# A statistics pass over scattered edge rows: all seven tile sums on TensorE, and six load buffers instead of four

## The reference, cut to what matters

```
def _bn(x, gamma, beta):
    mu = jnp.mean(x, axis=0)
    var = jnp.mean(jnp.square(x - mu), axis=0)
    return gamma * (x - mu) * jax.lax.rsqrt(var + EPS) + beta
z = jnp.concatenate([node_feats[src], node_feats[dst], edge_feats], axis=1)
gate = jax.nn.sigmoid(_bn(z @ W_int + b_int, g_int, be_int))
upd = jax.nn.softplus(_bn(z @ W_upd + b_upd, g_upd, be_upd))
agg = jax.ops.segment_sum(gate * upd, dst, num_segments=N_NODES)
```

## Time and profile before

| what | before |
|---|---|
| median of 3 runs | 12183.24 us |
| the profiled execution | 12194.69 us (span 12193.1) |
| busy over the span | DVE 75%, PE 65%, ACT 54%, POOL 42% |
| first to last v of the statistics stage (288 steps) | 3474.64 to 4572.85 us |
| in 3500 to 4500 us: DVE, PE, ACT busy of 1000 us | 955.6, 633.7, 585.1 us |
| in 3500 to 4500 us: granted TensorE clock, DMA | 1.00, 0.76 busy, 210 GB/s |

### The profile page before, as it was taken

The page is one execution under the profiler, slowest core; times in us unless marked ns, Lnnn a source line. Parts: engine busy times, 40 slices in busy tenths (PEclk is TensorE's granted clock), DMA queues, the critical chain, the costliest instruction groups (busy, mean ns, idle before and its releaser), DMA issues. The chain is left out here.

```text
span 12193.1 us, 449789 instructions
## 1 busy us (share of the span) xinstructions
PE 7964.7 (65%) x149683; PEld 7351.9 (60%) x149684; DVE 9105.9 (75%) x22324; ACT 6577.3 (54%) x15886; POOL 5172.2 (42%) x4482
## 2 busy tenths in 40 slices
PE   6444444388866667996676667667667676675865
PEld 6333333388854447886666666657666576665765
DVE  6777777578889999996785676875767757678367
ACT  1222222189965557995414545976458764588320
POOL 2777777634410001110360482643835527446044
PEclk8555555599999998997987867878678786787997
DMA  5555553289977777995994998969989799998897
GB/s 202 170 168 168 168 156 84 55 306 349 348 230 212 207 212 258 322 322 196 355 296 175 317 289 274 318 204 315 290 269 320 213 315 287 263 324 248 325 340 222
DMA packets 1409651, 3076.60 MB, mean 252 GB/s; under 512 B 389771, under 2 KB 1007813, under 8 KB 1398307
## 3 DMA queue, kind: packets, MB, share of 16 engines
q1 hardware_dynamic: 1034062, 2124.82, 50.1%
q0 software_dynamic: 331264, 823.09, 25.3%
q10 hardware_dynamic: 44116, 125.96, 3.4%
HBM read 1869.12 MB, written 1138.02 MB: 247 GB/s over the span
## 5 line engine op out<-in xcount | busy, mean ns | idle before, releaser
L2122 POOL DMA_INDIRECT mask_cols<-cols_all,mask_index x864 | 1372.5, 1589 | 1226.5 <-ACT mask_index L2131 1051.8
L539 POOL DMA_INDIRECT rows_s<-place_rec,place_index x1568 | 1635.7, 1043 | 538.5 <-issue 533.1
L614 PE MATMUL place_slot_ps<-place_runs,place_oh_turned 50*128 50x100 f32 x3136 | 725.9, 423 | 1236.8 <-DVE place_runs L653 1218.3
L614 PEld LDWEIGHTS place_slot_ps<-place_runs,place_oh_turned 50*128 50x128 f32 x3136 | 683.0, 327 | 1271.1 <-issue 1270.8
L2270 POOL DMA_INDIRECT hop_x<-cols_all,hop_index x864 | 976.2, 1130 | 1064.6 <-ACT hop_index L2277 741.2
L2286 ACT ACTIVATE hop_parts<-hop_x,mask 128x64 f32<-128x64 f32 x5184 | 1266.4, 335 | 51.0 <-DMA hop_x<-cols_all,hop_index 27.0
L2333 PE MATMUL hop_sums_ps<-hop_parts,hop_onehot 128*128 128x64 bf16 x18144 | 882.1, 216 | 470.3 <-DVE hop_parts L2315 394.3
L2333 PEld LDWEIGHTS hop_sums_ps<-hop_parts,hop_onehot 128*128 128x128 bf16 x18144 | 781.2, 113 | 573.6 <-issue 573.0
L1515 POOL DMA_DIRECT2D cm_onehot<-hot_d x288 | 152.1, 528 | 1978.1 <-POOLq L107 1180.2
L2180 PE MATMUL mask_part_ps<-mask_now,mask_turned 128*128 128x64 bf16 x18144 | 922.2, 233 | 33.2 <-issue 17.5
L2180 PEld LDWEIGHTS mask_part_ps<-mask_now,mask_turned 128*128 128x128 fp8e4 x18144 | 898.0, 125 | 38.1 <-issue 38.0
(11 more groups left out here) (411 smaller groups left out, 26855.7 us busy)
## 6 DMA issues: line engine op xcount, KB each, us to landing
cols_all<-att_in_rows SPq DMA_DIRECT2D x216, 896.0 KB
mask_onehot<-hot_s SPq DMA_DIRECT2D x216, 896.0 KB
cols_all<-hop_in_rows SPq DMA_DIRECT2D x216, 896.0 KB
hop_onehot<-hot_s SPq DMA_DIRECT2D x864, 224.0 KB
rows_all<-blank SPq DMA_DIRECT2D x72, 1808.0 KB
ct_u<-rows_all SPq DMA_DIRECT2D x288, 452.0 KB
cm_v<-rows_all SPq DMA_DIRECT2D x288, 448.0 KB
cm_onehot<-hot_d POOLq DMA_DIRECT2D x288, 448.0 KB
```

The source lines that it names most:

```text
L539: nc.gpsimd.indirect_dma_start(m.rows_s.rearrange("p n w -> (p n) w"), bass.IndirectOffsetOnAxis(index[:, j, t:t + 1], 0), rec[:, j, t, :] ...
L614: last = nc.tensor.matmul(slot_ps[b][:, t, 0:2 * NBK], oh_turned[:, b, t, :], runs[:, b, t, :], start=True, stop=True)
L2122: nc.gpsimd.indirect_dma_start(cols[:, n, :], None, table, bass.IndirectOffsetOnAxis(index[:, n, :], 0), compute_op=ALU.add).then_inc(arri ...
```

## The change

The sum of v goes to TensorE in full. `add_up` issues two identity products: tiles 0 to 3 (512 columns), and tiles 4 to 6 (384 columns), the latter into the first three of the same four places of one PSUM bank. VectorE's addition into `sum_acc` is gone, with its semaphore `summed` and the memset. `sum_acc` has four places instead of seven and is copied once from PSUM at the end, and `stage_gate_norm` sums four places of it. The loads go into six buffers of `u`, and the load for batch `it + 6` (instead of `it + 4`) waits for the same square. Six is not a multiple of the unrolling by four, so VectorE, ScalarE and SyncE go through `each12`; TensorE stays with `each4`.

```
-                    for c in range(BATCH):
-                        last = nc.tensor.matmul(ps[:, i, 0:2 * F], m.ones[:], acc[:, c, :], start=c == 0, stop=c == BATCH - 1)
+                    places = acc.shape[1]
+                    for c in range(places):
+                        last = nc.tensor.matmul(ps[:, i, 0:2 * F], m.ones[:], acc[:, c, :], start=c == 0, stop=c == places - 1)
...
-        u = sb("u", [P, 4, UW])
+        u = sb("u", [P, 6, UW])
...
+        came = [sem(f"came{n}") for n in range(6)]
+        total_ps = ctx.enter_context(nc.psum_tensor("ct_total_ps", [P, 512], fp32))[:].rearrange("p (c w) -> p c w", w=W)
...
-                    if isinstance(it, int):
-                        return
-                    sp.wait_ge(squared, it + 3)
-                    load(it + 4, i)
-                for i in range(4):
-                    load(i, i)
-                each4(sp, step)
+                    if look_ahead(it, 6):
+                        sp.wait_ge(squared, it + 3)
+                        load(it + 6, (s * 4 + i) % 6)
+                for n in range(6):
+                    load(n, n)
+                each12(sp, step)
...
-                nc.vector.memset(sum_acc[:], 0.0).then_inc(summed, 1)
...
-                def hots(it, i, k):
-                    dve.wait_ge(came[i], k * 16 + 16)
-                    dve.wait_ge(hot_stored[i], k * 16 + 16)
+                def hots(it, n, k):
+                    i = n % 4
+                    dve.wait_ge(came[n % 6], (k * 2 + n // 6) * 16 + 16)
+                    dve.wait_ge(hot_stored[i], (k * 3 + n // 4) * 16 + 16)
...
                     add_squares(it - 1, (i - 1) % 2)
-                    dve.wait_ge(valued, it + 3)
-                    dve.wait_ge(summed, it + 1)
-                    dve.sem_inc(gate, 1)
-                    nc.vector.tensor_tensor(sum_acc[:, 0:OWN, :], sum_acc[:, 0:OWN, :], v[:, i % 2, 0:OWN, :], ALU.add).then_inc(summed, 1)
...
                 dve.wait_ge(totaled, IT + 3)
-                nc.vector.tensor_copy(sum_acc[:, OWN:BATCH, :], total_ps)
+                nc.vector.tensor_copy(sum_acc[:], total_ps)
...
-                    nc.tensor.matmul(total_ps.rearrange("p c w -> p (c w)"), m.ident[:], v[:, j, OWN:BATCH, :].rearrange("p c w -> p (c w)"),
-                                     start=False, stop=False).then_inc(totaled, 1)
+                    nc.tensor.matmul(total_ps.rearrange("p c w -> p (c w)"), m.ident[:], v[:, j, 0:4, :].rearrange("p c w -> p (c w)"),
+                                     start=False, stop=False)
+                    nc.tensor.matmul(total_ps[:, 0:BATCH - 4, :].rearrange("p c w -> p (c w)"), m.ident[:],
+                                     v[:, j, 4:BATCH, :].rearrange("p c w -> p (c w)"), start=False, stop=False).then_inc(totaled, 1)
...
-                    sum_acc, square_acc = sb("sum_acc", [P, BATCH, 2 * F], ctx=stats), sb("square_acc", [P, BATCH, 2 * F], ctx=stats)
+                    sum_acc, square_acc = sb("sum_acc", [P, 4, 2 * F], ctx=stats), sb("square_acc", [P, BATCH, 2 * F], ctx=stats)
```

More of the change, by code:

```diff
@@ L1319, in stage_conv_stats @@
         v_ps = [ctx.enter_context(nc.psum_tensor(f"ct_v_ps{j}", [P, 8, W], fp32))[:, 0:BATCH, :] for j in range(2)]
[L1320 to L1325, removed]
+        came = [sem(f"came{n}") for n in range(6)]
+        hot_stored, turned_stored = sem4("hot_stored"), sem4("turned_stored")
+        hot, turn, turned_s, spread, valued, squared, added, totaled, gate = (sem(n) for n in (
+            "hot", "turn", "turned_s", "spread", "valued", "squared", "added", "totaled", "gate"))
+        total_ps = ctx.enter_context(nc.psum_tensor("ct_total_ps", [P, 512], fp32))[:].rearrange("p (c w) -> p c w", w=W)
         with nc.Block() as block:
@@ L1328, in _, with load, step @@
             def _(sp):
-                def load(it, i):
-                    sp.dma_start(u[:, i, :], m.rows_d[:, bass.ds(it, 1), :].rearrange("p b w -> p (b w)")).then_inc(came[i], 16)
-                def step(it, i, k, more, s):
+                def load(it, n):
+                    sp.dma_start(u[:, n, :], m.rows_d[:, bass.ds(it, 1), :].rearrange("p b w -> p (b w)")).then_inc(came[n], 16)
+                def step(it, s, i, k, more, _):
                     sp.wait_ge(hot, it + 1)
@@ L1354, in _ @@
                 nc.vector.memset(square_acc[:], 0.0).then_inc(added, 1)
-                nc.vector.memset(sum_acc[:], 0.0).then_inc(summed, 1)
                 nc.vector.memset(square[:, 1, :, :], 0.0).then_inc(added, 1)
-                def hots(it, i, k):
-                    dve.wait_ge(came[i], k * 16 + 16)
-                    dve.wait_ge(hot_stored[i], k * 16 + 16)
+                def hots(it, n, k):
+                    i = n % 4
+                    dve.wait_ge(came[n % 6], (k * 2 + n // 6) * 16 + 16)
+                    dve.wait_ge(hot_stored[i], (k * 3 + n // 4) * 16 + 16)
                     dve.sem_inc(gate, 1)
-                    nc.vector.tensor_tensor(onehot[:, i, :, :], b2(m.iota_p[:], BATCH), b3(u[:, i, C * W:C * W + C], P),
+                    nc.vector.tensor_tensor(onehot[:, i, :, :], b2(m.iota_p[:], BATCH), b3(u[:, n % 6, C * W:C * W + C], P),
                                             ALU.is_equal).then_inc(hot, 1)
@@ L1369, in add_squares, with step @@
                     nc.vector.tensor_tensor(square_acc[:], square_acc[:], square[:, j, :, :], ALU.add).then_inc(added, 1)
-                def step(it, i, k, more, s):
+                def step(it, s, i, k, more, _):
+                    n = s * 4 + i
                     if look_ahead(it, 2):
-                        hots(it + 2, (i + 2) % 4, k + (i + 2) // 4)
+                        hots(it + 2, (n + 2) % 12, k + (n + 2) // 12)
                     dve.wait_ge(spread, it + 1)
@@ L1377, in step @@
                     dve.sem_inc(gate, 1)
-                    nc.vector.tensor_tensor(v[:, i % 2, :, :], v_ps[i % 2][:], u[:, i, 0:C * W].rearrange("p (c w) -> p c w", w=W),
+                    nc.vector.tensor_tensor(v[:, i % 2, :, :], v_ps[i % 2][:], u[:, n % 6, 0:C * W].rearrange("p (c w) -> p c w", w=W),
                                             ALU.add).then_inc(valued, 1)
                     add_squares(it - 1, (i - 1) % 2)
-                    dve.wait_ge(valued, it + 3)
-                    dve.wait_ge(summed, it + 1)
-                    dve.sem_inc(gate, 1)
-                    nc.vector.tensor_tensor(sum_acc[:, 0:OWN, :], sum_acc[:, 0:OWN, :], v[:, i % 2, 0:OWN, :], ALU.add).then_inc(summed, 1)
                 hots(0, 0, 0)
                 hots(1, 1, 0)
-                each4(dve, step)
+                each12(dve, step)
                 add_squares(IT - 1, 1)
                 dve.wait_ge(totaled, IT + 3)
-                nc.vector.tensor_copy(sum_acc[:, OWN:BATCH, :], total_ps)
+                nc.vector.tensor_copy(sum_acc[:], total_ps)
             @block.scalar
@@ L1403, in turn_out, with step @@
                     nc.scalar.copy(turned[:, i, :, :], turn_ps[:], saturate=False).then_inc(turned_s, 1)
-                def step(it, i, k, more, s):
+                def step(it, s, i, k, more, _):
                     if more:
-                        turn_out(it + 1, (i + 1) % 4, k + (i + 1) // 4)
+                        turn_out(it + 1, (i + 1) % 4, k * 3 + s + (i + 1) // 4)
                     act.wait_ge(valued, it + 3)
@@ L1410, in step @@
                     act.sem_inc(gate, 1)
-                    nc.scalar.copy(m.map_d[:, bass.ds(it, 1)], u[:, i, C * W + C:UW])
+                    nc.scalar.copy(m.map_d[:, bass.ds(it, 1)], u[:, (s * 4 + i) % 6, C * W + C:UW])
                     nc.scalar.square(square[:, i % 2, :, :], v[:, i % 2, :, :]).then_inc(squared, 1)
@@ L1417, in _ @@
                 turn_out(0, 0, 0)
-                each4(act, step)
+                each12(act, step)
             @block.tensor
```

## The result

| | before | after |
|---|---|---|
| median | 12184.12 us (6 runs, 12174.13 to 12208.0) | 11989.67 us (6 runs, 11981.62 to 11995.35) |
| ratio to before | | 0.9838, 95% interval 0.9827 to 0.9848 |
| span of the profiled execution | 12193.1 us | 11980.0 us |
| first to last v of the stage | 3474.64 to 4572.85: 3.83 us a step | 3464.94 to 4360.51: 3.12 us a step |

The kernel is 194 us faster by the medians, 185 to 211 by the interval; 207 were forecast, to 11976 us. In the profiled executions the 287 steps from first to last v take 1098.2 - 895.6 = 202.6 us less. From the first load to the first v it is 0.2 us more (10.19 and 10.42), and from the last v to the multiplication by `bn_scale` behind the stage 2.3 less (14.48 and 12.18), in all 204.7 us less. The stage started 9.9 us earlier, though nothing ahead of it had changed.

The account below looks back on a forecast made before the run. The ring of four load buffers (3.77 us a step) was taken to bound, VectorE (3.62) close behind. A step of 3.11 saves 205.6 us, plus 1.1 at the end: 207 us, to 11976 us; range 11945 to 12055.

Parts of the forecast that it names:

- The ring of four: Four load buffers: a load waits for the square of four batches earlier, holding the step at 3.77 us or more.
- VectorE's new floor: VectorE's instructions in a step without the sum: 3.62 us falls to 3.01.
- TensorE's step: TensorE's work in a step: turn_in 0.39, spread 1.17 and add_up 1.49, in all 3.05 us.
- P: Time of one step of the stage: highest floor 3.05 plus 0.06, so 3.11 us; range 3.01 to 3.20.
- The store of the one-hot: A one-hot waits until its buffer, one of four, is stored: 3P >= 4.12 + L, giving 2.71 us a step.
- L: Time from issue of a one-hot's store to the start of its reader, taken as the load's 4.01 us.
- this rival: DMA engines or the one-hot's store become the bound: priced at 3.4 us a step, 123 us saved, chance 0.13.
- TensorE is the longest by a hair: After the change TensorE's 3.05 us a step stands just above VectorE's 3.01.
- one of the signs that I gave for being wrong on the mechanism: VectorE waiting for a DMA in front of the one-hot would show the mechanism wrong.
- DMA share: Busy share of the DMA engines in the stage after the change: 0.85 to 0.97 expected.
- the rival on TensorE's clock: TensorE partly at 1.2 GHz in the stage: at one half of the steps 4.58 us, 12398 us; chance 0.03.
- the 81 ns: Rival: TensorE's short products take 81 ns each in an unbroken stream: step 3.82 us, 3 us saved, chance 0.02.

Follow-up runs that it names:

- experiments 1 and 2: Changed kernel with VectorE's sum put back: 12125.45 us, ratio 0.995; kernel before with all sums on TensorE, still four load buffers: 12185.59 us, ratio 0.9998.
- experiment 4: Changed kernel without the 384-column product (tiles 4 to 6 unsummed) and with each one-hot stored one step earlier: 11940.89 us, ratio 0.9806 to the kernel before.
- experiment 3: Changed kernel without the 384-column product, so tiles 4 to 6 are missing from the sum: 11979.12 us, ratio 0.9829 to the kernel before.
- experiment 5: Changed kernel with only the store of each one-hot moved one step earlier: 11980.84 us, ratio 0.9844 to the kernel before.

## Why the prediction was right, and which of its steps were not

**The bound before: right.** "The ring of four at 3.77 and VectorE at 3.62" is what experiments 1 and 2 found: 3.81 with VectorE relieved alone, 3.60 with the ring of six alone. It was read from a wait of 39 us in 900 that looks like a detail, because the timeline shows which load it ends on the earlier trace rows.

**VectorE's new floor: right.** 3.01 forecast, 3.00 in experiment 4.

**TensorE's step: mis-sized.** The forecast had `add_up` at 1.49 us; it is 1.56, and the step 3.12, not 3.05. I took the pitch of a pass as 0.86 - 0.54 = 0.32. But 0.86 is the first pass's pitch plus the second pass's duration, and that duration, 0.486, is not the first one's 0.54. The first pass has a pitch of 0.86 - 0.486 = 0.375. The mean of 517 ns over the group, between the two, was the hint in the trace of before. I then added 0.06 for jitter, of which there is none on a full TensorE. Two errors of the same size cancelled: P = 3.11 forecast, 3.12 measured. That the step came out within 0.01 was luck.

**The store of the one-hot: the step that failed.** I took L as 4.01, the load's, "since both go through one queue", and got a harmless 2.71. The stage at its new pace has L at 5.3 on the mean of the one-hots that wait, and 4.12 + 5.3 over three steps is 3.14; over all steps, with those that don't wait, it held 3.10 (experiment 3). The row of before was that of a load, with the engines busy 0.76; the forecast needed that of a store behind such a load, at 0.95. Which of the two makes up the 1.3 us no run shows, because before no one-hot waited for its store. I had named this rival with the right mechanism and priced it at 3.37, on the assumption that it would stand above TensorE. It stands level with it. The Trainium skill, "DMA: Bandwidth & Descriptors", section "Latency and other measured facts", with its latency that grows under load, had led to an estimate of 5.8 for L; the 5.3 measured are nearer to that than to my 4.01. That it is the latency of the memory that grew is not shown by any run.

**What it means for the reasoning.** "TensorE is the longest by a hair" was right as a number and misleading as a picture. The prediction said that VectorE's idle time would stand in front of v. Most of what the groups show is in front of the one-hot, 8.9 us against 1.4, and the part that has a name is put down to a DMA. That was one of the signs that I gave for being wrong on the mechanism, and it came. What saves the forecast is experiment 5: with that wait gone the step stays at 3.12, so TensorE does bound the changed kernel.

**The rest.** DMA share 0.95, within 0.85 to 0.97. The granted clock in the stage was 1.00: the rival on TensorE's clock didn't come. The short products stay 56 ns apart in an unbroken stream, 1.17 us for 21 of them, so the 81 ns of the Trainium skill, "TensorE: Matmul & The Clock Gate", section "Back-to-back issue gap", don't hold for these products: TensorE is full, and its step is 3.12, not 3.76. The sums over partitions gave 2.3 us, not 1.1: I had the count of passes right, 14 to 8, but their 0.188 us was a pitch at a granted clock of 0.60. At 1.00 it is 0.97 / 8 = 0.121, and the passes of `square_acc`, which I had left alone, became shorter too. The stage's 895.6 us lie just outside the 890 to 895 I named. The 207 us forecast lie inside the measured interval of 185 to 211, and the stage with its edges, 204.7 us less, is nearer to them than the medians are.

## What to carry to other kernels

A short wait in front of the busiest engine can be the real bound: follow it to the issue that it ends on and write the circle down, with the number of steps it spans. If two limits lie within a few per cent, each half of a change measures as little or nothing, and only both together pay. When a change drives the DMA engines from 0.76 to 0.95 busy, don't carry over a latency read at the old share, least of all one of another transfer; moving one issue ahead of a wait in the issuing engine's order is a cheap repair, but it pays only where nothing else holds the step (0.10 us a step in experiment 4, nothing in experiment 5). And take a pitch from two starts, not from the difference of two durations.

## What the runs showed of the hardware that I had not expected

- The first f32 pass behind bf16 and fp8 products costs about 0.06 us more than the ones behind it, for 384 (recorded 0.54 against 0.49), 448 (0.59 against 0.54) and 512 columns (0.65 against 0.59).
- From the issue of a 224 KB store to the start of what waits for it took 5.3 us on the mean with the DMA engines 95% busy, the store standing right behind a load of 452 KB.
- The busy share of the DMA engines followed the pace of the steps and was no limit of its own: 0.76 at 210 GB/s, 0.95 at 258 and 0.96 at 269, which is 2.9 to 3.0 us busy a step each time. The floor of 2.94 us was not reached; the shortest step was 3.00.
- The same 14 f32 passes of 128 columns took 2.37 us at a granted clock of 0.72 and 1.73 at 1.00, though nothing in them had changed: how long they take hangs on the clock that is granted there.
- An f32 addition of 384 columns on GpSimd beside VectorE lengthened the VectorE instruction that started while it ran by 0.80 us, one of 128 columns by 0.26; the additions themselves took 1.64 and 1.10.
